# Second attention of a two-layer gated cross-attention block: the first score block ahead of the next pair's maxima, in 26 of 31 passes

## The reference

```python
q = lat @ Wq
kv = jnp.concatenate([x, lat], axis=1) @ Wkv
k, v = jnp.split(kv, 2, axis=-1)
...
dots = jnp.einsum('bhid,bhjd->bhij', q, k) * scale
attn = jax.nn.softmax(dots, axis=-1)
out = jnp.einsum('bhij,bhjd->bhid', attn, v)
return out.transpose(0, 2, 1, 3).reshape(b, m, heads * dim_head) @ Wout
...
x = x + jnp.tanh(g_xattn[1]) * _L1_xattn_ref(ctx_1024, _layernorm(x), ...)
```

## Time and profile before

| | us |
|---|---|
| median of 3 runs | 777.44 |
| lowest, highest | 772.36, 777.78 |
| the profiled execution | 777.46 |
| its span, first to last instruction | 775.7 |
| TensorE (matmuls) busy | 720.0 (93%) |
| VectorE busy | 556.0 (72%) |
| ScalarE busy | 358.5 (46%) |
| GpSimd busy | 334.4 (43%) |

### The profile page before, as it was taken

The page is one execution under the profiler, slowest core; times in us unless marked ns, Lnnn a source line. Parts: engine busy times, 40 slices in busy tenths (PEclk is TensorE's granted clock), DMA queues, the critical chain, the costliest instruction groups (busy, mean ns, idle before and its releaser), DMA issues.

```text
span 775.7 us, 14479 instructions
## 1 busy us (share of the span) xinstructions
PE 720.0 (93%) x5654; PEld 537.4 (69%) x5654; DVE 556.0 (72%) x1086; ACT 358.5 (46%) x530; POOL 334.4 (43%) x411
## 2 busy tenths in 40 slices
PE   5779999999999998999999999999999989999996
PEld 4656666666877776666776666766767656887794
DVE  4767887774887777886668767587966787677444
ACT  2657767665434335545544555345454545120300
POOL 3283534410333114666556566566665674100000
PEclk9779999999999999999999999999999999999999
DMA  8100000000500040000000000000000000000000
GB/s 178 17 1 2 3 1 2 2 2 9 210 1 0 1 106 4 2 2 1 2 1 1 2 2 2 1 2 1 1 2 1 2 1 1 1 8 1 8 8 7
DMA packets 25554, 11.57 MB, mean 15 GB/s; under 512 B 11832, under 2 KB 24200, under 8 KB 25360
## 3 DMA queue, kind: packets, MB, share of 16 engines
q1 hardware_dynamic: 24480, 10.59, 5.3%
q10 hardware_dynamic: 1008, 0.07, 0.1%
HBM read 10.06 MB, written 0.52 MB: 14 GB/s over the span
## 4 chain that ended last, share of the span: by engine, by line
PE 74%; DVE 18%; issue 4%; ACT 3%; DMA 1%; SPq 0%; DVEq 0%; ACTq 0%
PE ps L1689 71%; DVE o L1416 2%; PE ps L1700 2%; ACT v L598 1%; DVE mx L1092 1%; DVE pmax L1400 1%; DVE ysum L1548 1%; DVE pmax L1403 1%; DVE kql L1391 1%; DMA raw<-in_L_xattn_Wproj_dram 1%; DVE rs_t L962 1%; PE ps L1793 1%; DVE rs_t L969 1%; DVE cn L1353 1%; DVE xnC L1203 1%
## 5 line engine op out<-in xcount | busy, mean ns | idle before, releaser
L837 ACT ACTIVATE p<-ps 128x1024 f32<-128x1024 f32 x96 | 96.3, 1025 | 129.8 <-PE ps L1689 129.8
L573 POOL TENSOR_TENSOR acc<-p 128x256 f32<-128x256 f32 x128 | 92.7, 755 | 97.7 <-ACT p L837 97.7
L1689 PE MATMUL ps<-p,v 128*64 128x256 f32 (+1 forms) x1280 | 130.2, 386 | 1.8 <-DVE o L1417 1.3
L1689 PE MATMUL ps<-kqh 64*128 64x256 f32 (+1 forms) x640 | 105.1, 363 | 10.8 <-ACT v L598 4.6
L579 POOL TENSOR_TENSOR acc<-acc,p 128x256 f32<-128x256 f32 x128 | 89.8, 733 | 49.7 <-ACT p L837 49.7
L1400 DVE TENSOR_REDUCE pmax<-ps 128x2 f32<-128x1024 f32 x64 | 78.2, 1222 | 34.4 <-PE ps L1689 33.4
L1092 DVE TENSOR_REDUCE mx<-ps 128x1 bf16<-128x512 f32 x128 | 82.5, 687 | 26.5 <-PE ps L1689 25.9
L1689 PEld LDWEIGHTS ps<-p,v 128*64 128x64 f32 (+1 forms) x1280 | 63.3, 125 | 50.8 <-issue 18.8
L534 POOL TENSOR_SCALAR q<-qst,rmask 128x256 fp32r<-128x256 f32 x64 | 58.7, 936 | 59.3 <-ACT qst L598 59.3
L1689 PEld LDWEIGHTS ps<-kqh 64*128 64x128 f32 x640 | 58.9, 190 | 35.7 <-issue 29.1
L702 ACT ACTIVATE p<-ps 128x1024 f32<-128x1024 f32 x64 | 65.5, 1025 | 23.1 <-PE ps L1689 21.4
(11 more groups left out here) (285 smaller groups left out, 1593.4 us busy)
## 6 DMA issues: line engine op xcount, KB each, us to landing
w<-in_L_ffn_W_dram SPq DMA_DIRECT2D x1, 2048.0 KB, 12.1
wt<-in_L_ffn_W_dram SPq DMA_DIRECT2D x4, 512.0 KB, 6.2
ctx_all<-in_ctx_dram SPq DMA_DIRECT2D x4, 256.0 KB, 5.7
raw_kv<-in_L_xattn_Wkv_dram SPq DMA_DIRECT2D x1, 1024.0 KB, 4.9
raw<-in_L_ffn_B_dram SPq DMA_DIRECT2D x9, 64.0 KB
xr<-in_x_dram SPq DMA_DIRECT2D x4, 128.0 KB, 4.0
raw_q<-in_L_xattn_Wq_dram SPq DMA_DIRECT2D x1, 512.0 KB, 5.9
wout<-in_L_xattn_Wout_dram SPq DMA_DIRECT2D x1, 512.0 KB, 7.2
```

Of the source, the lines that this page charges most:

```text
L573: ins = pool.tensor_tensor(acc1[:, at], p1[:, s, 0, at], p1[:, s, 1, at], ALU.add)
L837: act.activation(p1[:, g % 2, u, :], bank(2 * (n % 2), 2), ACT.Exp, scale=SCALE1).then_inc(a_exp1.sem, 1)
L1689: return pe.matmul(o, lhsT, rhs, start=start, stop=stop)
```

## The change

A flag `m_taken` is true in pass g when the pass before put a value tile in bank 5. In these passes `scores1(g, 0)` goes ahead of `max1(g + 1, 0)`, and `project(g + 3, 0)` ahead of `max1(g + 1, 1)`. The other passes, and the programs of the other engines, are as before.

```diff
@@ -2323,19 +2323,24 @@
 
             for g in range(G1 + 1):
                 b, p = divmod(g, NPAIR)
+                m_taken = g >= 1 and values_use(g - 1) is not None
                 if g < G1:
-                    if g + 1 < G1:
+                    if g + 1 < G1 and not m_taken:
                         max1(g + 1, 0)
                     scores1(g, 0)
+                    if g + 1 < G1 and m_taken:
+                        max1(g + 1, 0)
                     if g == G1 - 3:
                         turned_in1(0)
                     if g == G1 - 2:
                         probs1(0)
                     scores1(g, 1)
-                    if g + 1 < G1:
+                    if g + 1 < G1 and not m_taken:
                         max1(g + 1, 1)
                     if g + 3 < G1:
                         project(g + 3, 0)
+                    if g + 1 < G1 and m_taken:
+                        max1(g + 1, 1)
                     if g == G1 - 3:
                         head1(0)
                     if g == G1 - 1:
```

## The result

| | before | after |
|---|---|---|
| median | 775.1 (11 runs) | 781.75 (11 runs) |
| lowest, highest | 772.16, 779.48 | 778.03, 782.81 |
| profiled execution, its span | 777.46, 775.7 | 782.17, 780.4 |

The ratio is 1.0072, 95% interval 1.0051 to 1.0092, so 5.6 us by the ratio; the two medians lie 6.65 us apart. The forecast was 782.9. It had been added to 777.46 us, and the median of before came down to 775.1 with more runs, so that the 1.1 us between 782.86 and 781.75 are what is left of a starting value 2.4 too high and a step 1.2 too small against the medians. The nearness of the two times is thus partly luck; what can be judged is the step of 5.4.

A forecast was written before the change was run, and what follows sets the result against it. TensorE's own stream was taken to bound the second attention. The terms -0.1 - 2.1 + 3.0 + 3.2 + 1.4 gave +5.4 us on 777.46, so 782.9 us, with a range of 773.5 to 788.

The forecast's parts named there:

- What bounds: Second attention: TensorE's own stream is the time, busy 339.03 of 353.00 us; distances between blocks matter, not busy time.
- Regular pairs: 14 pairs with a second value tile in bank 7: removed wait and extra change of shape cancel, -0.01 each, -0.1 us.
- Pairs 2, 28, 29: Nothing in bank 7 behind the value tile: the long wait for ScalarE's copy goes, -0.70 each, -2.1 us.
- Output product: Pairs 10, 18, 26: projection waits for `xr`, which stands behind the later first reduction on VectorE; +1.0 each, +3.0 us.
- Latents: Pairs 5, 13, 21: projection waits for `kv_t` of the turned latents, behind the later first reduction; +0.48 each, +1.4 us.
- Context: Pairs 4, 12, 20: VectorE, already late, frees bank 7 later still and the projection waits; +1.07 each, +3.2 us.
- The term for VectorE's lateness: Context pairs: `kql` of the pass ahead must follow the second maxima's reduction, so VectorE comes 0.63 us later.
- The faster one: Rival: bank 7 does not hold the projection, so the nine pairs behave as regular ones; -3.7, 773.8 us; chance 0.10.
- the nine waits: Idle time of 0.7 to 1.7 us expected ahead of the projection in context, latents and output product pairs.
- The slower one: Rival: the extra change of shape costs a whole weight load, 0.19 us in each of 26 pairs; 787.8 us; chance 0.14.
- The one in between: Rival: pluses and minuses cancel, the nine waits being half of what was worked out; +1.6, 779 us; chance 0.12.
- the nine terms: Losses forecast where VectorE must free bank 7: output product +3.0, context +3.2, latents +1.4 us, three pairs each.

The follow-up runs named there:

- E2: Kernel after with `max1(g + 1, 0)` back ahead of `scores1(g, 0)`, so only the projection is moved; 783.15 us, 1.0081 of before.
- E7: Before with the new order only in pairs 2, 28, 29, 11 regular and three latents pairs, the latents' read-out ahead of the first reduction; 770.66 us, ratio 0.9921.
- E4: Kernel after with VectorE's read-outs of bank 7 ahead of its reduction of the first maxima; 772.09 us, 0.9934 of before.
- E8: Kernel after with `proj_low(g + 3, 1)` ahead of `second_slot(g)` in passes 3, 11, 19; 777.91 us, 1.0018 of before.

## Why the prediction was right, and where it was off

- **What bounds.** TensorE's stream, and in it the distances: the pairs' changes add up to 5.44 of the 5.4 forecast; its busy time moved by 1.9 of 720. That the sum is so close is in part luck: the context pairs gave +3.5 instead of +3.2 and the latents +1.2 instead of +1.4, and before had none of its context pairs late in the execution that is compared.
- **Regular pairs, -0.01.** Measured -0.02 to -0.03 in twelve, +0.04 in pair 3, +0.19 in pair 1; the 14 together -0.08 instead of -0.1. That gain and extra change of shape cancel was shown by E2 (+0.20 for the change of shape alone). Pair 1 was counted with them and lost 0.19; the change of shape was paid there with nothing to remove. E7 leaves it as before and it went back to 11.88.
- **Pairs 2, 28, 29, -0.70.** Measured -0.66, -0.72, -0.76.
- **Output product, +1.0.** Measured +1.00 three times, through the chain M0, reduction, `xr`, P0. Shown by E4, where that order alone is undone.
- **Latents, +0.48.** Measured +0.43 and +0.37. The mechanism is the same; P0 came 3.53 us behind the transposes (437.35 to 440.88) instead of the 3.63 of the forecast.
- **Context, +1.07.** Measured +1.18. The term for VectorE's lateness was mis-sized and wrongly composed. I had 0.63 for it; the reduction started 3.81 behind the maxima row instead of 3.03, 0.78. The later `kql` of pass 11 came as worked out (0.52 by the maxima row), but the `cn` after it took 1.68 instead of 1.96 and gave 0.28 of it back; the collision with GpSimd in `max_cols` and `xnC` added 0.43. So most of the right size came from something that the prediction did not know. And `kql` of the second half, 0.67 late, holds up the transposes, a wait that the prediction did not name; through M0 it adds the last 0.11. P0's idle time was 1.08, not the 1.6 that the prediction expected there, since TensorE had already stood 0.68 ahead of the transposes.
- **The rivals.** The faster one falls with the nine waits, 8.0 us. The slower one falls with the handovers of 0.33 and 0.43, under its own limits of 0.45 and 0.55. The one in between falls with the size of the nine terms. The clock stayed at 1.00 through the second attention:

```profile
292.00:650.00 358.00, 341.90 (x3224) 238.38 (x3221) 258.79 (x350) 172.76 (x242) 219.73 (x285) 1.00 0.01 1
```

- **What stays open.** Whether E4 and E7 give as much as their medians say. Against 777.2 of before on their chip they are 5.1 and 6.5 us faster, and in the pairs 2.51 and 3.25. The low ends of their intervals are 2.6 and 3.7 us (777.2 x 0.0034 and x 0.0048), just above what the pairs show, and the clock, below, adds steps of its own. Whether these would even out with more runs was not tried. Nor is it known what sends the first `cn` one way or the other.

## What to carry to other kernels

When a block is moved so that a wait disappears, follow the bank or buffer that the block *behind* it needs to whoever frees it, and look at what stands ahead of that release on the other engine: here a read-out that had been ready for 1.4 us stood behind a reduction that the move delayed. Move both orders together, or only where nothing has to be freed: the same idea cost 5.4 us in all 26 pairs, and gave 3.3 in the 17 that could take it, the latents' read-out moved along (E7). Putting a block of another shape into this stream cost 0.2 us each time, as much as the wait that it was to remove. And look at the forecast of each group of pairs beside its measured value: a sum can be right with two of its terms off.

## What the hardware did that was not expected

**One operation of 0.34 or 0.92 us sets 0.66 us.** With the same order of instructions, and starts that agree within 0.02 us, VectorE's first `cn` in pass 3, 11 or 19 takes 0.34 or 0.92; with it `max_cols` comes ahead of GpSimd's `acc` or behind it and takes 0.18 or 0.60 us, and the context pair behind it 11.54 or 12.20. Five of 15 went the long way.

**Stretches at half clock come and go.** Between the two attentions the granted clock falls from 2.4 to 1.2 GHz in single short stretches, and their number differs by execution: TensorE's program is the same there, and it was busy for the same 59.7 us of the 65 in all four kernels below. The window from 205 to 270 us of before, the repeat of before, E7 and E8 in turn (the first figure behind the five busy times is the granted clock; 1.00 is 2.4 GHz):

```profile
205.00:270.00 65.00, 59.71 (x271) 50.10 (x271) 53.89 (x180) 24.92 (x38) 17.38 (x13) 0.95 0.00 1
```

```profile
205.00:270.00 65.00, 59.71 (x268) 50.16 (x267) 52.39 (x168) 25.59 (x39) 18.27 (x13) 0.92 0.00 1
```

```profile
205.00:270.00 65.00, 59.71 (x283) 50.38 (x282) 55.07 (x173) 27.12 (x42) 20.37 (x15) 0.97 0.00 1
```

```profile
205.00:270.00 65.00, 59.74 (x290) 50.73 (x289) 56.50 (x174) 27.12 (x42) 20.38 (x15) 1.00 0.00 1
```

The stretch between the maxima rows on either side took 116.11, 117.61, 114.51 and 112.78 us in these, with 2, 3, 1 and 0 stretches at half clock in it: steps of 1.5 to 1.7, one for each. All eleven profiles fit: 112.78 with none, 114.5 with one, 116.1 with two, 117.6 with three. Behind the second attention it is the same, 138.9 us with one such stretch and 140.4 to 140.5 with two. That makes up much of the spread of 7 us among runs of before, and is why the pairs' distances tell more here than one profiled time.
